# Two-layer gated cross-attention kernel: which engine reads the second half of the transposed tokens in the second layer

## The reference

```python
x = x + tanh(g_xattn[0]) * L0_attention(layernorm(x), ctx, ...)
x = x + tanh(g_ffn[0])   * L0_ffn(layernorm(x), ...)
x = x + tanh(g_xattn[1]) * L1_attention(layernorm(x), ctx, ...)   # the second layer's attention
x = x + tanh(g_ffn[1])   * L1_moe(layernorm(x), ...)              # 8 experts, top 2

def L1_attention(x, context):            # 16 heads of 64
    q = x @ Wq                           # needs layernorm(x) with the features on the partitions
    k, v = split(context @ Wkv)
    k, v = concat(null_k, k), concat(null_v, v)
    attn = softmax(q @ k.T / 8)
    return layernorm(attn @ v @ Wout) * ln_scale + ln_bias
```

## Time and profile before

| | us |
|---|---|
| median of 3 runs | 1890.05 (1887.49 to 1890.36) |
| the profiled execution | 1889.55 |
| its span, first to last instruction | 1887.7 |
| PE busy in the span | 1762.2 (93%) |
| DVE busy | 1213.7 (64%) |
| ACT busy | 1113.1 (59%) |
| POOL busy | 459.5 (24%) |

### The profile page before, as it was taken

How to read it: one execution, slowest core, us unless ns; L and a number is a source line. 1 busy time by engine, 2 the same in 40 slices (tenths; PEclk the granted TensorE clock), 3 DMA queues, 4 the chain that set the end, 5 groups by cost and what they waited for, 6 DMA issues and landing times. The chain is left out here.

```text
span 1887.7 us, 28143 instructions
## 1 busy us (share of the span) xinstructions
PE 1762.2 (93%) x9516; PEld 1114.1 (59%) x9516; DVE 1213.7 (64%) x2860; ACT 1113.1 (59%) x2332; POOL 459.5 (24%) x434
## 2 busy tenths in 40 slices
PE   5799998898899899999999999999988889999997
PEld 3455554455454444444544464445446889999997
DVE  3867876876877576455456455645764876666664
ACT  2467666666667656555455545554564656766664
POOL 2101111110120010000000002000203677777775
PEclk8899999999999999999999999999999999999999
DMA  3000000010003048000000000100007568667660
GB/s 101 1 23 1 1 23 1 1 29 1 1 1 134 1 155 253 1 23 1 1 1 23 1 1 24 34 1 12 24 13 241 161 194 224 192 194 226 196 196 6
DMA packets 123054, 128.12 MB, mean 68 GB/s; under 512 B 10912, under 2 KB 118304, under 8 KB 122912
## 3 DMA queue, kind: packets, MB, share of 16 engines
q1 hardware_dynamic: 114176, 117.65, 19.9%
q0 software_dynamic: 8160, 8.67, 2.5%
q10 hardware_dynamic: 576, 0.00, 0.0%
HBM read 97.43 MB, written 30.69 MB: 68 GB/s over the span
## 5 line engine op out<-in xcount | busy, mean ns | idle before, releaser
L1155 DVE TENSOR_REDUCE l_tile_max<-psum 128x1 f32<-128x512 f32 x512 | 341.9, 688 | 110.4 <-PE psum L833 108.6
L1003 ACT ACTIVATE l_probs<-psum 128x1024 f32<-128x1024 f32 x256 | 248.2, 1022 | 106.8 <-PE psum L845 103.3
L2578 POOL TENSOR_TENSOR moe_w_lo<-moe_w,moe_w_hi 128x512 fp32r<-128x512 f32 x184 | 260.1, 1414 | 122.3 <-ACT moe_w_hi L2360 120.5
L1911 DVE TENSOR_REDUCE l_row_max<-psum 128x2 f32<-128x1024 f32 x124 | 151.7, 1223 | 205.2 <-PE psum L1566 204.6
L833 PE MATMUL psum<-l_kT,l_qT 128*128 128x512 f32 x512 | 238.1, 472 | 40.1 <-DVE l_tile_max L1155 36.8
L2290 PE MATMUL psum<-moe_xs_hi,moe_w_hi 128*128 128x256 f32 x736 | 212.4, 289 | 2.6 <-DVE moe_xs_lo L2410 2.6
L2290 PE MATMUL psum<-moe_xs_lo,moe_w_hi 128*128 128x256 f32 x736 | 210.1, 286 | 0.0
L2290 PE MATMUL psum<-moe_xs_hi,moe_w_lo 128*128 128x256 f32 x736 | 209.9, 285 | 0.0
L833 PEld LDWEIGHTS psum<-l_kT,l_qT 128*128 128x128 f32 x512 | 98.3, 193 | 131.7 <-DVE l_tile_max L1155 111.0
L1754 ACT ACTIVATE l_probs<-psum,l_neg_max 128x512 f32<-128x512 f32 x248 | 167.2, 674 | 0.0
L845 PE MATMUL psum<-l_qT,l_kT 128*128 128x512 f32 x512 | 161.1, 399 | 1.5 <-ACT l_probs L1003 1.5
(11 more groups left out here) (323 smaller groups left out, 3290.5 us busy)
## 6 DMA issues: line engine op xcount, KB each, us to landing
moe_w<-in_moe_w SPq DMA_DIRECT2D x276, 256.0 KB, 4.6
moe_sorted_x<-l_zeros SPq DMA_DIRECT2D x1, 17680.0 KB, 56.0
moe_xs<-moe_sorted_x SPq DMA_DIRECT2D x23, 272.0 KB
moe_w<-in_ctx SPq DMA_DIRECT2D x8, 512.0 KB, 3.7
moe_w<-in_ctxT SPq DMA_DIRECT2D x4, 1024.0 KB, 5.6
moe_w<-in_wkv SPq DMA_DIRECT2D x2, 2048.0 KB, 15.6
x_resid<-in_x SPq DMA_DIRECT2D x4, 512.0 KB, 10.1
out_x<-x_resid SPq DMA_DIRECT2D x4, 512.0 KB
```

The lines of the kernel that those rows point to most:

```text
L1003: nc.scalar.activation(probs[:, n % PT_RING], wide(2 * (n % 2)), ACT.Exp, scale=SCALE).then_inc(exp_done, 1)
L1155: nc.vector.reduce_max(tile_max[:, q % 2, t, h, half:half + 1], bank(max_bank(m)), AX_X).then_inc(max_read, 1)
L1911: nc.vector.reduce_max(row_max[:, t, :], wide(2 * (t % 2)).rearrange("p (j m) -> p j m", j=2), AX_X)
L2578: nc.gpsimd.tensor_tensor(w13_lo[:, k % SPLITS], w13[:, slot_k, :, cols], w13_hi[:, k % SPLITS].bitcast(F32), ALU.subtract).then_inc(w13_s ...
```

## The change

`read_by_dve` no longer names half 1 of every batch, only that of the opening stage (`("xT", 0, 1)`, which stays in the table because the counts begin there). ACT's `read_fill` already has a branch for `xT`; DVE's loses its own. So for i = 5, 13 and 21 ACT copies half 1 where its own walk through the table comes to `(i, 3, 0)`: ahead of `exponentials(i + 1, 3)`. PE's wait before the query projection is on ACT's counter instead of DVE's.

```diff
     def read_by_dve(fill):
-        return fill[0] in ("k", "null", "logits", "prefix") or fill[0] == "xT" and fill[2] == 1
+        return fill[0] in ("k", "null", "logits", "prefix") or fill == ("xT", 0, 1)
 
@@ in layer1, DVE's read_fill
                         if i >= 2:
                             dve.wait_ge(s_psum, (i - 1) * T)
                         last = nc.vector.tensor_copy(k_sb[:, i % 2, :], bank(MISC))
-                    elif kind == "xT":
-                        last = nc.vector.tensor_copy(xT[:, rest[1], :], bank(MISC))
                     elif kind == "logits":
                         last = router.add_bias(bank(MISC))
```

## The result

| us | before | after |
|---|---|---|
| median, 11 runs each on one chip | 1888.14 (1885.14 to 1895.35) | 1877.75 (1873.35 to 1885.35) |
| profiled execution, its span | 1889.55, 1887.7 | 1878.52, 1876.8 |

The ratio after to before is 0.9947 with a 95% interval of 0.9930 to 0.9964: 10 us won, between 6.8 and 13.2. Forecast were 6.3 us won, a time of 1883.5 and a range of 1880.7 to 1888.0. The kernel before came out at 1888.14, where the prediction started from 1889.8; that is 1.7 us of the miss. The other 4.1 us are a larger gain: 10.4 us between the medians.

The account below looks back on a forecast made before the run. PE was taken to set the pace. Gains of 1.94 + 2.2 + 2.2 = 6.3 us at three places give 1883.25 from the profiled 1889.55, 1883.75 by the runs' median; predicted 1883.5, range 1880.7 to 1888.0.

Parts of the forecast that it names:

- PE bounds, the wait is all its idle time: Batch from 794 us: PE busy 193.13 of 195.00 us; its 1.87 us idle is the query projection's wait for DVE's copy.
- The wait that goes (1.94, 2.50, 2.50): Query projection at three second-layer places: starts later than the ordinary 1.06 us behind its scores, by these us.
- what is late next (2.2 kept): Probability transposes behind the projection wait for DVE's last normalization: 1.94 us stay at the first place, 2.2 at each other.
- ACT's copy costs nothing: At the three places, ACT's 0.60 us copy of half 1 fits its idle wait for DVE's maxima; cost nothing.
- The cover: ACT's idle time before the exponentials hides its copy of half 1, with some 0.3 us to spare.
- Everything behind moves up as a whole: After the three places, the rest of the program hangs on PE's progress and moves up by the full 6.3 us.
- The waits of 1.9 and 2.4 us at the three places cost no clock, so there is nothing to win there: Query projection's waits: granted clock was 1.00 in the batch from 794 us, so no clock gain was counted.
- Rival 3: Behind 1200 us, shifted gaps bring further clock drops, making the kernel slower; four give 1895.5 us; chance 0.04.
- more than 7.5 us, by a clock drop saved: Whole program: a gain above 7.5 us because a clock drop is saved; chance 0.03.
- The size given to a low stretch, 3 us: Read behind the 3.04 us wait at 1408.91: one stretch of PE at low clock costs about 3 us.

Follow-up runs that it names:

- e1: The change at the first place only, DVE still copying half 1 at the second and third, against the kernel before: one execution, 1889.76 us.
- f1: Kernel before with PE's four transposes of half 0 for the last batch repeated 3 more times, 1.3 us added work: median 1891.86 us, ratio 1.0010.
- f2: Kernel before with PE's four transposes of half 0 for the last batch repeated 5 more times, 2.2 us added work: median 1889.22 us, ratio 1.0003.
- c_before: The kernel before, unchanged, timed against itself: median 1889.65 us against 1889.54, ratio 1.000.
- e5: Kernel before with DVE's copy of half 1 made three times, ready 1.5 us later: one execution, second layer's stretch 759.8 us against 750.3.
- c_before_2: The kernel before, unchanged, run once more for its trace: second layer's stretch 749.9 us.
- c_after: The changed kernel, unchanged, timed again against the kernel before: median 1880.03 us, ratio 0.9955.
- c_after_2: The changed kernel, unchanged, timed a third time against the kernel before: median 1880.86 us, ratio 0.9941.
- e3: Changed kernel with ACT's copy of half 1 preceded by a second into an unread spare buffer: one execution, second layer's stretch 743.0 us against 744.0.

## Why the prediction was right, and where it failed

- **PE bounds, the wait is all its idle time**: right. Its idle time in the batch went from 1.87 to 0 us.
- **The wait that goes (1.94, 2.50, 2.50)** and **what is late next (2.2 kept)**: right. Measured 1.94, 2.35 and 2.35, 6.6 us against the sum's 6.3.
- **ACT's copy costs nothing**: right; a doubled copy showed it. The cover was 0.31 us, as forecast.
- **Everything behind moves up as a whole**: right in the first pair of traces (0.1 us between the third place and the end). In others the experts' part was 4.1 to 5.0 us longer or shorter with the same instructions, by the clock and the wait that came with it.
- **"The waits of 1.9 and 2.4 us at the three places cost no clock, so there is nothing to win there"**: this is the step that failed. The sum put the clock behind these waits at nothing, by one execution, in which it was true. Over the six traces with such waits at their old length (three of the kernel before, e1, f1 and f2) there are 17 waits, and 5 have a low clock behind them (c_before 2, e1 1, f1 1, f2 1), each costing 1.6 to 1.7 us. The seven traces without these waits have none in 21 places, and e5, with longer ones, has 3 in 3. On average that is 3 x 5/17 x 1.65 = 1.5 us for the change, which makes 6.6 + 1.5 = 8.1 us; 5 cases of 17 fix the share only roughly. Together with the start that was 1.7 us too high and the waits' 0.3 us this accounts for 3.5 of the 5.8 us by which the forecast was missed. The other 2.3 us have no cause that was shown; the first comparison's interval of 6.8 to 13.2 us holds 8.1.
- **Rival 3 and the range**: the mechanism that I allowed for slower runs, clock drops behind waits, worked in the other direction, since the change takes waits away. I gave "more than 7.5 us, by a clock drop saved" a chance of 0.03. Its proper place was in the forecast itself. The size given to a low stretch, 3 us, was wrong too: at the three places it was 1.6 to 1.7 us, and near 1409 us, where it was read, next to nothing. c_before_2 kept the clock there, was 1.5 us further at the layer's last L1697 and only 0.3 us at the start of the experts (749.9 against 750.3), where PE waits for the transfer. The Trainium skill (TensorE: Matmul & The Clock Gate, section What's actually happening) says that the monitor runs free and does not start anew with the kernel. The traces agree with that but do not prove it: the same wait of 2.44 us costs the clock in one execution and not in another.
- **The rest stays partly open.** All runs together give 1888.75 (87 runs of the kernel before, mean) and 1879.45 (23 of the change), 9.3 us, known to about 1.5 us by the spread of the runs; the shifted changed kernels, relative to the kernel before on their chip and less their added work, give 6.7 and 6.7, known to 2.6 and 1.7 us. 8.1 lies between and within all three. That the changed kernel's own position in time gives it the short experts' part more often (theory E) stays possible and is not shown.

## What to carry to other kernels

An instruction that another engine waits for should not stand in its own engine's queue behind work that waits for a third; moving the copy ahead of that work gave 5.5 of the 6.6 us, the other engine the last 1.1. It was not that DVE was the fuller engine: in the first of these batches ACT was busier (105.78 against 100.94 us of 195). Count a wait of PE at its length plus a share of what the clock costs behind it, even if the one trace at hand shows the clock at full: waits of 1.9 to 2.4 us cost 1.65 us more in 5 of 17 cases, waits of 3.4 to 4.0 us 1.6 us more in 3 of 3. Before a stretch is priced, see what PE waits for behind it: in front of the transfer at the start of the experts 1.5 us won were worth 0.3. And changes of a few us cannot be told from one profile: compare stretch by stretch, and keep the stretches that the change does not touch out of the sum.

## What the runs showed of the hardware that was not expected

The granted clock after one and the same wait differs from execution to execution: behind the 3.04 us wait near 1409 us it fell in the first trace of both kernels and stayed at 1.00 in c_before, c_after, c_before_2, c_after_2, e3 and f2; behind 2.44 us it fell in some and not in others. One execution's first layer took 684.4 us, another's of the same instructions 688.8. And a low stretch can draw another after it: the one behind the 2.56 us wait in the experts' part was made up within 6 us, but a second wait of 2.5 us with a low clock followed, and the two together made that part 4.1 to 5.0 us longer.
